# Three steps of the third group moved earlier in the passage between two stages of a kernel on one core

## The reference, cut to what matters

```python
x = x + _L0_gnn_ref(_layernorm(x), adj, ...)      # normalized adjacency, one aggregation
x = x + _L0_ffn_ref(_layernorm(x), ...)           # one matmul
x = x + _L1_gnn_ref(_layernorm(x), adj, ...)      # convolutions, distances, gates r, z, n
x = x + _L1_ffn_ref(_layernorm(x), ln_w, ln_b, W, b)

def step(h, _):                                   # the last one, 30 times
    h = h + 0.01 * jnp.tanh(h)
    h = h * jax.nn.sigmoid(h)
    h = _layernorm(h, ln_w, ln_b)
    h = jnp.einsum('bsc,dc->bsd', h, W) + b
    return (h, None)
```

## Time and profile before

| | us |
|---|---|
| median of 3 runs | 1262.13 (1261.93 to 1262.24) |
| profiled execution, time | 1262.43 |
| profiled execution, span | 1260.7 |

### The profile page before, as it was taken

One profiled execution on the slowest core, in us unless ns is written; L12 is line 12 of the kernel. 1 busy time (PEld: TensorE's weight loads), 2 busy tenths in 40 slices (PEclk: granted clock), 3 DMA queues, 4 the chain that ended last, 5 costly groups with the idle time before them and its releaser, 6 DMA issues.

```text
span 1260.7 us, 27945 instructions
## 1 busy us (share of the span) xinstructions
PE 1227.7 (97%) x9073; PEld 1094.8 (87%) x9073; DVE 1151.1 (91%) x3026; ACT 961.3 (76%) x1174; POOL 950.1 (75%) x668
## 2 busy tenths in 40 slices
PE   7899999999999999879999999999999999999998
PEld 6677777777777777669999999999999999999998
DVE  7988888888888887799999999999999999999996
ACT  2455555555555555779999999999999999999994
POOL 2455555555555555589999999999999999999996
PEclk9999999999999999979999999999999999999999
DMA  6111111111111100000000000000000000000004
GB/s 197 43 43 42 43 42 42 42 42 42 42 42 42 41 0 1 1 1 1 1 0 0 0 0 0 0 0 0 0 0 0 0 0 0 0 0 0 0 0 134
DMA packets 29814, 27.78 MB, mean 22 GB/s; under 512 B 3286, under 2 KB 21465, under 8 KB 29657
## 3 DMA queue, kind: packets, MB, share of 16 engines
q1 hardware_dynamic: 29784, 27.41, 6.9%
HBM read 23.21 MB, written 4.19 MB: 22 GB/s over the span
## 4 chain that ended last, share of the span: by engine, by line
PE 47%; DVE 3%; issue 2%; POOL 2%; ACT 1%; DVEq 0%; POOLq 0%
PE psum L907 28%; PE psum L959 15%; PE psum L924 3%; POOL h_ring L543 2%; DVE u_ring L1360 1%; ACT t_ring L1026 1%; DVE f_share L1397 1%; DVE f_stat L1343 1%; DVE psum L1402 0%; DVE psum L1413 0%; DVE psum L1416 0%; DVE f_rs L1431 0%; DVEq L389 0%; DVE y_all L1365 0%; DVEq L1341 0%
## 5 line engine op out<-in xcount | busy, mean ns | idle before, releaser
L543 POOL TENSOR_TENSOR h_ring<-g_pair,f_rs 128x1024 f32<-128x1024 f32 x240 | 452.4, 1906 | 31.2 <-DVE f_rs L1431 18.6
L1343 DVE BATCH_NORM_STATS2 f_stat<-g_pair 128x6 f32<-128x256 f32 x960 | 396.1, 427 | 2.4 <-ACT g_pair L1016 2.4
L959 PE MATMUL psum<-ident,h_ring 128*128 128x128 f32 (+1 forms) x1920 | 297.2, 277 | 4.1 <-POOL h_ring L543 3.1
L1360 DVE SCALAR_TENSOR_TENSOR u_ring<-t_ring,psum 128x1024 f32<-128x1024 f32 x232 | 282.3, 1217 | 5.7 <-issue 2.3
L959 PEld LDWEIGHTS psum<-ident,h_ring 128*128 128x128 f32 (+1 forms) x1920 | 248.1, 167 | 31.4 <-issue 3.7
L907 PE MATMUL psum<-w1c_t,y_all 128*128 128x128 f32 x1920 | 254.7, 276 | 0.0
L1030 ACT ACTIVATE y_all<-psum 128x1024 f32<-128x1024 f32 x240 | 243.9, 1016 | 14.1 <-PE psum L959 14.1
L907 PE MATMUL psum<-w_t,y_all 128*128 128x128 f32 x1920 | 254.5, 276 | 0.0
L1016 ACT ACTIVATE g_pair<-u_ring 128x1024 f32<-128x1024 f32 x240 | 251.7, 1049 | 0.0
L1026 ACT ACTIVATE t_ring<-psum 128x1024 f32<-128x1024 f32 x232 | 238.0, 1026 | 16.2 <-PE psum L907 9.6
L907 PEld LDWEIGHTS psum<-w1c_t,y_all 128*128 128x128 f32 x1920 | 234.6, 193 | 0.0
(11 more groups left out here) (203 smaller groups left out, 2148.2 us busy)
## 6 DMA issues: line engine op xcount, KB each, us to landing
work<-in_adj_dram SPq DMA_DIRECT2D x16, 1024.0 KB, 5.5
x_tok<-in_x_dram SPq DMA_DIRECT2D x16, 256.0 KB, 5.6
out_dram<-y_all SPq DMA_DIRECT2D x7, 512.0 KB, 3.2
work<-in_L_gnn_conv_w_dram SPq DMA_DIRECT2D x1, 1088.0 KB
out_dram<-y_all SPq DMA_DIRECT2D x2, 256.0 KB, 3.6
work<-in_L_gnn_w_ih_dram SPq DMA_DIRECT2D x1, 384.0 KB
work<-in_L_gnn_w_hh_dram SPq DMA_DIRECT2D x1, 192.0 KB
work<-in_L_gnn_W_dram SPq DMA_DIRECT2D x1, 64.0 KB, 5.4
```

Source lines behind the costliest of these rows:

```text
L543: pool.tensor_tensor(tiles(h_ring[j % 4]), tiles(g_ring[j]), spread(f_rs[:, both(j), at:at + GT], GT, C), ALU.mult).then_inc(f_norm, 1)
L959: m = pe.transpose(g_ps[j % 2][0:rows, t // NT, P * (t % NT):P * (t % NT) + P], tiles(h_ring[j % 4])[:, t, 0:rows], ident[:])
L1343: ins = dve.bn_stats(f_stat[:, j, 0, 2 * q:2 * q + 2, :].rearrange("p t w -> p (t w)"), two)
L1360: dve.scalar_tensor_tensor(out=u_ring[k % 2], in0=t_ring[k % 2], scalar=STEP, in1=src, op0=ALU.mult, op1=ALU.add).then_inc(f_u, 1)
```

## The change

Five steps change places; none is added or removed.

- ACT, last graph (`b == B - 1`): the silu of group 2 now stands ahead of the tanh of group 3 (it stood behind `gh_n`).
- DVE, same step: the statistics of group 2 and its variance now stand ahead of the sum of group 3 (the statistics stood behind it, the variance in the next step ahead of the sum of group 4).
- POOL, next step (`b == B`): the scaling of group 2 now stands ahead of the last graph's root (it stood behind it).

```diff
--- before.py
+++ after.py
@@ -592,10 +592,10 @@
                 if ends(b, B):
                     power(2)
                     centre_one(2)
+                    scale(0, 2, 2)
                 if later(b) and not ends(b, B - 1):
                     rstd(3, b - 1)
                 if ends(b, B):
-                    scale(0, 2, 2)
                     centre_one(3)
                     power(3)
@@ -1135,6 +1135,7 @@
                 if ends(b, B - 1):
+                    silu(2, 2)
                     tanh(0, 3)
@@ -1146,8 +1147,6 @@
-                if ends(b, B - 1):
-                    silu(2, 2)
@@ -1510,7 +1509,6 @@
                 if ends(b, B):
-                    variance(2)
                     scaled_sum(0, 4)
@@ -1605,8 +1603,9 @@
                 if ends(b, B - 1):
                     variance(0)
                     variance(1)
+                    statistics(2, 2)
+                    variance(2)
                     scaled_sum(0, 3)
-                    statistics(2, 2)
```

## The result

| | median us | range | runs |
|---|---|---|---|
| before, beside the changed kernel | 1262.03 | 1260.95 to 1262.91 | 12 |
| changed | 1264.66 | 1264.25 to 1265.63 | 12 |

The ratio is 1.0023, 95% interval 1.0015 to 1.003: 2.6 us slower, 0.5 us beyond the upper end of the range. The profiled execution of the changed kernel took 1264.55 us with a span of 1262.7.

What follows compares the result with a forecast made beforehand. PE alone bounds the end from 555.67, fed by two paths, POOL's and `upd`-PE-ACT-DVE sum. +0.82 (`upd`) - 0.80 (transposes, bias) = +0.02 us, half counting: 0, so the median, 1262.1 us; range 1260.2 to 1264.2.

Steps and rivals of the forecast that it cites:

- What bounds it: Before group 2's bias at 556.8: two paths, POOL's and DVE `upd` -> PE -> ACT -> DVE sum; shortening one leaves the other.
- ACT, the fourth sum and `upd`: ACT loses nothing; on DVE the moved fourth sum meets POOL's first scaling, so L1494 and `upd` come 0.82 us late.
- the first rival: On DVE, L1494 goes straight behind the fourth sum, ahead of POOL's waiting scaling: `upd` 1.3 us early, 1261.1 us; chance 0.17.
- the first step that failed: On POOL, third power to end of fourth scaling loses two meetings, 0.9 us each: ends 553.1, before group 7's sum.
- the third rival: Group 7's sum waits for POOL's fourth scaling, up to 1.2 us, and the clock may return later: 1264.4 us; chance 0.13.
- The -0.80 us of PE: On PE, transposes and bias done before the sum or at full clock: 1.46 us from 556.82 to 558.28 become 0.66.
- Half of that for the end: On PE, a shift at the lower clock counts half at the end, both kernels running low until about 561.6.
- the first forecast sum: At group 2's product on PE: +0.82 through `upd` less 0.80 for transposes and bias, +0.02 us, counted as 0.

Runs made afterwards that it cites:

- POOL's part and the variance: Kernel before with the third group's variance right behind its statistics and its scaling ahead of the last root, fourth sum, silu and statistics unmoved: ratio 1.0010, +1.61 us.
- `upd` ahead of the fourth sum: Changed kernel with the fourth sum and the norm of graph 14 moved behind `upd` on DVE: 1263.60 us, ratio to the kernel before 1.0013.
- keeping the clock up: Extra matmuls in PE's idle time before group 3's transposes: 20 on the changed kernel, ratio to before 1.0005; 13 on the kernel before, 0.9995.
- POOL's part alone: Kernel before with only the third group's scaling moved ahead of the last root on POOL: 1264.68 us, ratio 1.0024.
- the third power first: Kernel before with early variance, third group's power ahead of the second scaling, and that scaling held until `upd` is there: ratio 0.9985, -1.75 us.
- POOL's part alone and the fourth scaling held: Kernel before with the third group's scaling ahead of the last root, and the fourth scaling held until group 7's sum is done: ratio 1.0010, +1.15 us.

## Why the prediction was wrong

In short: the forecast had the fourth scaling out of the way of the sum of group 7 and took 0.80 us off for a full clock at the bias. The sum stood 1.08 us behind the scaling, the clock had fallen before the bias, and the delay of 1.88 us counted in full.

**What bounds it: right.** There were two paths to the bias, and the one over `upd`, ACT and DVE's sum is what PE waited for (3.30 us at L924). In the nine kernels whose clock was left alone the first table's last two columns go together, from -1.6 to +2.7 us of bias. An earlier fourth scaling alone bought nothing: in the changed kernel it ended 1.0 us earlier on the anchor, with POOL's part and the variance 1.8 us, with `upd` ahead of the fourth sum 1.3 us, and all three are slower than the kernel before.

**ACT, the fourth sum and `upd`: right in mechanism and size.** The sum took 1.51 us, L1493 waited for the scaling (2.38 us), and the waiting POOL, not the next DVE instruction, had its turn: the first rival is out. Forecast +0.82 us on `upd`, measured +0.80.

**POOL: the first step that failed.** I took the earlier end of its range for the fourth scaling, because two meetings (0.9 us each) would fall away. They did shrink, the power by 0.47 us and the scaling by 0.88, and so did two others, the third scaling (2.28 to 1.90) and the fourth group's centring (2.10 to 1.04). But three came: the root beside the sum of group 5 (2.02 - 1.01), the fourth power beside the sum of group 6 (2.69 - 1.64) and 0.25 us on the third group's centring, 2.3 us in all. From the third power to the end of the fourth scaling it was 13.3 us, where 13.6 were read and 11.8 forecast. On the anchor the scaling ran from 17.64 to 19.54 us; I had put its start at 16.2 to 18.0 and chosen about 16.2. Moving work on POOL does not remove meetings, it deals them anew, and each instruction, the small ones too, had to be laid against each sum. So the third rival's meeting happened: given 0.13, and priced at 1.2 us on the sum (measured 1.08). It turned on the scaling starting after 551.5, and my own range for that start was 551.2 to 553.0, nearly all of it behind that point: the meeting should have been the likelier case. That the rival's 1264.4 us lies near the 1264.66 measured is partly luck: it counted the delay by half and added 1.7 us for a low stretch half as long again, while in the profiles the low stretch was 6.8 us before and after.

**The -0.80 us of PE: the second step that failed.** Bias and last transposes were to run at the full clock, in 0.66 us. PE had stopped at 554.9, the clock fell at 557.6, before the bias at 558.24, and from the bias to the product it was 1.45 us as before. The rows spoke against the term: there the clock fell 2.3 us after PE stopped (552.5 to 554.8), and with the early scaling that I chose, PE would have stopped at about 553.9 and paused 3.7 us before the bias. Whether the clock would still have been full after a shorter pause, had the second meeting not come, no run shows.

**"Half of that for the end": the third.** I let a delay at the lower clock count half, since the low stretch would end at 561.6 whatever happened. Over the ten profiles it ended at 558.4 to 565.7, 2.4 to 6.2 us after the bias, and at one length of the low stretch the delay of the bias reaches the end at about its full length. Half was too little; as the first forecast sum had only 0.02 us to halve, this alone would have changed nothing there.

With the rows as read, the two meetings at their full length would have given 1262.03 + 0.80 + 1.08 = 1263.9. The other 0.75 us are not shown apart. They fit a longer low stretch in more of the executions (granted clock 0.991 to 0.993 in all twelve of the changed kernel, 0.991 to 0.996 with the median 0.994 before), and keeping the clock up takes 1.9 us off the changed kernel and only 0.74 off the one before.

## What to carry to other kernels

Where two engines exclude one another at a port, the order of the work on one of them can be what keeps the other's critical instruction free: before moving anything, write down for every instruction behind the move which instruction of the other engine it will now stand beside, and who comes first. Where the other engine's path sets the end, let the one with slack wait on purpose (a semaphore ahead of a long instruction; here 2.15 us of idle time on POOL took 1.5 us off the changed kernel), or put work there that does not hold the port (the third power in the second scaling's place, 1.75 us off the kernel before). Count a delay of TensorE's restart at its full length until a run shows otherwise, and do not take the length of a low stretch from one profile.

## What the runs showed of the hardware

- In these records a start less than 0.1 us earlier does not always win the port. POOL's scaling started 0.05 us before DVE's instruction and waited for it (538.01 and 538.06 in the kernel before), likewise at 0.01 (546.20 and 546.21). At 0.09 us of lead it was DVE that waited, 1.7 us (553.98 and 554.07 in the kernel with POOL's part alone).
- A POOL instruction that already waits gets its turn between two DVE instructions that follow one another: the first scaling went behind the fourth sum, and L1493, next on DVE, took 2.38 us instead of 1.07.
- POOL's small instructions wait as well: the root of 128x4 took 2.02 us beside a sum instead of 1.01, the power of 128x8 2.69 instead of 1.64. A sum that started 0.10 us behind a power was not held up (530.29 and 530.39 in the kernel before): the sum took its usual 1.23 us and the power its least, 1.64. Nor were L1505, L1508 and L1511 (0.68, 0.69 and 0.69 us) beside the second of the two powers with the third power first, while those two powers together took 4.44 us.
- An fp32 matmul of 128x127 is two instructions of 0.11 us at the full clock (170 for 85, 19.0 us); a transpose is one (L959: four transposes, x4).
- The clock's low stretch behind this pause was 3.4 us long in four profiles, 6.8 in five and 10.2 in one (555.4 to 565.7 with POOL's part alone). It did not begin at a fixed time either: 2.3 us after PE had stopped in the kernel before (552.5 to 554.8), 4.8 us with POOL's part alone and the fourth scaling held (551.1 to 555.9).
